# Self-attention of the second layer: softmax weights normalised before the turn, values multiplied head by head in 32-column blocks

## The reference

```python
def _L1_attn_ref(x, Wq, Wkv_down, Wk_up, Wv_up, Wo):   # N_HEADS = 8, HEAD_DIM = 32
    q = (x @ Wq.T).reshape(b, t, 8, 32)
    kv_latent = x @ Wkv_down.T                          # 64 wide
    k = (kv_latent @ Wk_up.T).reshape(b, t, 8, 32)
    v = (kv_latent @ Wv_up.T).reshape(b, t, 8, 32)
    scores = einsum('bqhd,bkhd->bhqk', q, k) * 32 ** -0.5
    attn = softmax(scores, axis=-1)
    out = einsum('bhqk,bkhd->bqhd', attn, v).reshape(b, t, 256)
    return out @ Wo.T
```

## Time and profile before

| | |
|---|---|
| median of 3 runs | 5312.76 us (5300.98 to 5316.85) |
| the profiled execution's own time | 5294.46 us |
| its span, first to last instruction | 5292.7 us |
| busy share TensorE / VectorE / ScalarE / GpSimd | 89% / 61% / 40% / 35% |
| mean granted TensorE clock | 0.935 of full speed |
| the stage of the change | about 2130 to 2432 us of the span |

### The profile page before, as it was taken

The page is one execution under the profiler, slowest core; times in us unless marked ns, Lnnn a source line. Parts: engine busy times, 40 slices in busy tenths (PEclk is TensorE's granted clock), DMA queues, the critical chain, the costliest instruction groups (busy, mean ns, idle before and its releaser), DMA issues.

```text
span 5292.7 us, 138451 instructions
## 1 busy us (share of the span) xinstructions
PE 4721.4 (89%) x48761; PEld 3730.1 (70%) x48761; DVE 3207.9 (61%) x9513; ACT 2119.9 (40%) x5243; POOL 1841.9 (35%) x2796
## 2 busy tenths in 40 slices
PE   4999999999999999896929999777999989997999
PEld 3777777779867777674627777665577768885776
DVE  4777777756546666565425666685466657764443
ACT  1444444422224444221214555342255545542333
POOL 2555555511113333334143433890034434430000
PEclk8999999999989999896968999898899998888999
DMA  6000000000000000000220100002211100005665
GB/s 201 18 18 18 18 18 18 18 1 2 1 21 29 32 28 25 0 0 20 70 63 29 36 32 28 1 0 55 58 33 32 32 21 0 0 0 114 144 143 134
DMA packets 112436, 199.69 MB, mean 38 GB/s; under 512 B 13315, under 2 KB 54659, under 8 KB 111259
## 3 DMA queue, kind: packets, MB, share of 16 engines
q1 hardware_dynamic: 108147, 188.67, 13.4%
q0 software_dynamic: 4096, 8.40, 0.6%
HBM read 183.29 MB, written 18.97 MB: 38 GB/s over the span
## 4 chain that ended last, share of the span: by engine, by line
PE 75%; DVE 7%; issue 6%; ACT 5%; POOL 4%; SPq 1%; DMA 1%; POOLq 1%; DVEq 0%; ACTq 0%
PE psum_banks L555 6%; PE psum_banks L3075 6%; PE psum_banks L3084 5%; PE psum_banks L560 5%; PE psum_banks L620 4%; PE psum_banks L664 4%; PE psum_banks L671 3%; PE psum_banks L1623 3%; PE psum_banks L624 3%; PE psum_banks L1658 2%; PE psum_banks L2103 2%; PE psum_banks L1084 2%; PE psum_banks L2770 2%; PE psum_banks L1599 2%; ACT scratch L1741 1%
## 5 line engine op out<-in xcount | busy, mean ns | idle before, releaser
L787 DVE TENSOR_REDUCE scratch<-psum_banks 128x2 f32<-128x514 f32 x768 | 531.6, 692 | 411.8 <-PE psum_banks L555 407.8
L706 ACT ACTIVATE scratch<-psum_banks 128x512 f32<-128x512 f32 x768 | 459.4, 598 | 490.0 <-PE psum_banks L565 474.4
L560 PE MATMUL psum_banks<-scratch 32*128 32x128 f32 x6144 | 639.6, 310 | 8.2 <-ACT scratch L706 6.1
L555 PE MATMUL psum_banks<-scratch 32*128 32x257 f32 x3072 | 575.2, 441 | 50.3 <-DVE scratch L788 50.0
L560 PEld LDWEIGHTS psum_banks<-scratch 32*128 32x128 f32 x6144 | 476.6, 185 | 17.5 <-ACT scratch L706 8.6
L555 PEld LDWEIGHTS psum_banks<-scratch 32*128 32x128 f32 x3072 | 253.9, 189 | 272.7 <-issue 175.9
L3084 PEld LDWEIGHTS psum_banks<-w_L_ffn_down,scratch 128*128 128x128 f32 (+1 forms) x2560 | 335.8, 193 | 156.0 <-issue 127.1
L3075 PE MATMUL psum_banks<-scratch,w_L_ffn_up 128*128 128x512 f32 (+1 forms) x752 | 382.0, 603 | 8.2 <-DVE scratch L3262 8.2
L3262 DVE TENSOR_TENSOR scratch<-scratch 128x512 f32<-128x512 f32 x304 | 210.3, 692 | 268.5 <-ACT scratch L3128 234.3
L3128 ACT ACTIVATE scratch<-psum_banks 128x512 f32<-128x512 f32 x320 | 191.0, 598 | 430.1 <-PE psum_banks L3075 430.0
L565 PE MATMUL psum_banks<-shift_T,own_batch 32*128 32x128 bf16 x3072 | 351.2, 215 | 0.0
(11 more groups left out here) (495 smaller groups left out, 12386.3 us busy)
## 6 DMA issues: line engine op xcount, KB each, us to landing
scratch<-route_T SPq DMA_DIRECT2D x136, 512.0 KB, 7.3
scratch<-in_ctx SPq DMA_DIRECT2D x99, 514.0 KB, 3.5
scratch<-in_ctx_rows SPq DMA_DIRECT2D x130, 128.0 KB, 2.0
scratch<-route_T SPq DMA_DIRECT2D x8, 1024.0 KB, 8.8
expert_rows<-in_ctx SPq DMA_DIRECT2D x10, 512.0 KB, 17.9
scratch<-expert_rows SPq DMA_DIRECT2D x16, 192.0 KB, 2.7
expert_out<-scratch SPq DMA_DIRECT2D x16, 192.0 KB, 2.1
w_L_ffn_up<-in_L_ffn_up SPq DMA_DIRECT2D x1, 2992.0 KB
```

The source lines that it names most:

```text
L555: return pe.matmul(S[:, g % 2, :], qbd[q, t.odd, (s // 2) * P:(s // 2 + 1) * P], kT_of[q, t.odd, s // 2, :], start=True, stop=True)
L560: return pe.matmul(W[:, g % 2, c * P:(c + 1) * P], kT_of[q, t.odd, b, c * P:(c + 1) * P], qbd[q, t.odd, b * P:(b + 1) * P], start=True, st ...
L706: act.activation(pT[:, b % 2, 2 * h:2 * h + 2].rearrange("p t c q -> p t (c q)"), W, ACT.Exp).then_inc(exp_ready.sem, 1)
L787: dve.tensor_reduce(parts[:, r.t.odd, 2 * h:2 * h + 2, 0, b], S, X_AXIS, ALU.max, negate=True)
```

## The change

Four things, for L1 alone:

1. VectorE multiplies the exponentials by the inverse sums of their rows (256 columns, in place) before TensorE turns them. The tensor `w` and its instruction (L1302) are gone.
2. V becomes one matmul for each head and batch: 32 matmuls with a head's values of one batch (all 128 rows of the spread `vm`, 32 columns) at rest and 32 columns of turned weights moving. The four j's of a batch write to the four 32-partition parts of PSUM. The result already has the layout channel x token. Below it is called **V'**.
3. H and VectorE's L1268 are gone; ScalarE copies V's result (128x256) straight to `outT`, as soon as `pv_done` says that it is there.
4. In TensorE's round, TU moves from behind TX to behind S. M, V', TX, PJ, S, TU, OU is the new order.

```diff
         def values(t):
             pe.wait_ge(turned_read.sem, turned_read.at(t, 1))
             pe.wait_ge(vm_ready.sem, vm_ready.at(t, 1))
-            pe.wait_ge(heads_ready.sem, heads_ready.at(t + -1, 1))
+            if kind == "L1":
+                pe.wait_ge(heads_read.sem, heads_read.at(t + -1, 1))
+            else:
+                pe.wait_ge(heads_ready.sem, heads_ready.at(t + -1, 1))
             for n in range(nt):
                 left, vm = s["pT"][:, n * P:(n + 1) * P], s["vm"][:, t.odd, :]
                 if kind == "L1":
-                    mm = pe.matmul(O[n][:, :], left, vm[:, n * 512:(n + 1) * 512], start=True, stop=True)
+                    for b in range(NB):
+                        for j in range(4):
+                            d, q = slice(32 * j, 32 * j + 32), slice(n * P + 32 * j, n * P + 32 * j + 32)
+                            at = n * P + 32 * b
+                            mm = pe.matmul(O[0][d, at:at + 32], vm[:, n * 512 + b * P + 32 * j:n * 512 + b * P + 32 * j + 32],
+                                           s["pT"][:, q], start=True, stop=True, skip_group_check=True)
...
-            if kind == "L1" and r.own:
-                turn(r.t)
             if r.after:
                 project(r.t + 2)
...
-            if r.turned:
+            if kind != "L1" and r.turned:
                 heads(r.t + -1)
...
-            if kind == "L3" and r.own:
+            if kind != "L2" and r.own:
                 turn(r.t)
...
         def take_heads(t):
-            n = 2 if kind == "L1" else 1
-            act.wait_ge(heads_written.sem, heads_written.at(t, 1))
-            act.activation(s["outT"][:, 0:n, :], OUT[:, 0:n * P].rearrange("p (t c) -> p t c", t=n), ACT.Copy
-                           ).then_inc(heads_read.sem, 1)
+            if kind == "L1":
+                act.wait_ge(pv_done.sem, pv_done.at(t, 1))
+                act.wait_ge(out_written.sem, out_written.at(t + -1, 1))
+                act.activation(s["outT"], O[0][:, 0:2 * P].rearrange("p (t c) -> p t c", t=2), ACT.Copy).then_inc(heads_read.sem, 1)
...
-            heads(r)
...
-                link(dve.tensor_tensor(w, bc(s["rr"][:, 0:8], 2, 4), bc(k.c("quad"), 1, 8), ALU.mult), r, "w")
+                dve.tensor_tensor(by_head, by_head, bc(s["rr"][:, 0:8], 2, 32), ALU.mult).then_inc(probs_ready.sem, 1)
```

More of the change, by code:

```diff
@@ L894, in chain_steps @@
         if kind == "L1":
-            return (["max"] * has.own + ["stats"] * has.third + ["rs", "rr", "w"] * has.own)
+            return (["max"] * has.own + ["stats"] * has.third + ["rs", "rr"] * has.own)
         if kind == "L2":
@@ L908, in self_attention @@
     spread = PerTile(k.sig("operands_spread"), 1) if kind != "L1" else None
-    turned_written, turned_read, pv_done, heads_ready, heads_written, heads_read, out_written, out_read = (
-        PerTile(k.sig(n), 1) for n in ("probs_T_written", "probs_T_read", "pv_done", "heads_ready", "heads_written",
-                                       "heads_read", "out_written", "out_read"))
+    turned_written, turned_read, pv_done, heads_read, out_written, out_read = (
+        PerTile(k.sig(n), 1) for n in ("probs_T_written", "probs_T_read", "pv_done", "heads_read", "out_written", "out_read"))
+    if kind == "L1":
+        exp_ready = PerTile(k.sig("exp_ready"), 1)
+    else:
+        heads_ready, heads_written = PerTile(k.sig("heads_ready"), 1), PerTile(k.sig("heads_written"), 1)
     if kind == "L1":
@@ L1081, in heads @@
             pe.wait_ge(out_read.sem, out_read.at(t + -1, 1))
[L1082 to L1085, removed]
+            for b in range(NB):
+                mm = pe.matmul(OUT[:, 0:P], s["om"][:, 0, b * P:(b + 1) * P], window(k, b), start=(b == 0), stop=(b == NB - 1),
+                               skip_group_check=True)
             mm.then_inc(heads_written.sem, 1)
@@ L1090, in output @@
             if kind == "L1":
+                pe.wait_ge(out_read.sem, out_read.at(t + -1, 1))
                 for n in range(2):
@@ L1164, in take_heads @@
         def take_heads(t):
-            n = 2 if kind == "L1" else 1
-            act.wait_ge(heads_written.sem, heads_written.at(t, 1))
-            act.activation(s["outT"][:, 0:n, :], OUT[:, 0:n * P].rearrange("p (t c) -> p t c", t=n), ACT.Copy
-                           ).then_inc(heads_read.sem, 1)
+            if kind == "L1":
+                act.wait_ge(pv_done.sem, pv_done.at(t, 1))
+                act.wait_ge(out_written.sem, out_written.at(t + -1, 1))
+                act.activation(s["outT"], O[0][:, 0:2 * P].rearrange("p (t c) -> p t c", t=2), ACT.Copy).then_inc(heads_read.sem, 1)
+            else:
+                act.wait_ge(heads_written.sem, heads_written.at(t, 1))
+                act.activation(s["outT"][:, 0, :], OUT[:, 0:P], ACT.Copy).then_inc(heads_read.sem, 1)
         def one(r):
@@ L1208, in one @@
                     act.wait_ge(scores_read.sem, scores_read.at(r.t, 1))
-                    act.activation(s["pr"][:, 0:256], s["pr"][:, 0:256], ACT.Exp).then_inc(probs_ready.sem, 1)
+                    act.activation(s["pr"][:, 0:256], s["pr"][:, 0:256], ACT.Exp).then_inc(exp_ready.sem, 1)
             if kind == "L2" and r.own:
@@ L1260, in heads @@
             t = r.t + -1
-            if kind != "L1":
-                over_sums(r)
-            dve.wait_ge(pv_done.sem, pv_done.at(t, 1))
+            over_sums(r)
             dve.wait_ge(heads_written.sem, heads_written.at(t + -1, 1))
             w = s["w"].rearrange("p u j -> p (u j)")
[L1266 to L1270, removed]
+            dve.tensor_tensor(s["om"][:, 0, :].rearrange("p (g d) -> p g d", d=hd), O[0].rearrange("p (g d) -> p g d", d=hd),
+                              bc(w, 2, hd), ALU.mult).then_inc(heads_ready.sem, 1)
         def residual(r):
@@ L1280, in one_l1 @@
             sc, pr = D[:, 0:256].rearrange("p (u k) -> p u k", k=32), s["pr"][:, 0:256]
-            nm, w = s["nm"][:, 0:8], s["w"][:, 0:8, :]
+            nm = s["nm"][:, 0:8]
             normalised(r)
@@ L1298, in one_l1 @@
             if r.own:
-                dve.wait_ge(probs_ready.sem, probs_ready.at(r.t, 1))
-                link(dve.tensor_reduce(s["rs"][:, 0:8], pr.rearrange("p (u k) -> p u k", k=32), X_AXIS, ALU.add), r, "rs")
+                dve.wait_ge(exp_ready.sem, exp_ready.at(r.t, 1))
+                by_head = pr.rearrange("p (u k) -> p u k", k=32)
+                link(dve.tensor_reduce(s["rs"][:, 0:8], by_head, X_AXIS, ALU.add), r, "rs")
                 link(dve.reciprocal(s["rr"][:, 0:8], s["rs"][:, 0:8]), r, "rr")
-                link(dve.tensor_tensor(w, bc(s["rr"][:, 0:8], 2, 4), bc(k.c("quad"), 1, 8), ALU.mult), r, "w")
+                dve.tensor_tensor(by_head, by_head, bc(s["rr"][:, 0:8], 2, 32), ALU.mult).then_inc(probs_ready.sem, 1)
             residual(r)
```

## The result

The changed kernel takes 5351.68 us (median of four runs, 5348.12 to 5353.49) against 5306.87 us for the kernel before in the same session (5300.50 to 5316.85). The ratio is 1.0078, 95% interval 1.0064 to 1.0093: slower by 0.8%, 45 us. The forecast was 5363 us, by case A: TensorE at 1.2 GHz through the whole stage.

What follows compares the result with a forecast made beforehand. The prediction took TensorE, at its granted clock, to bound the stage. Thirty rounds at 1.2 GHz add 57.2 us and the stage's end saves 6.5, +50.7 on a median of 5312.76: 5363 us, 8 in 10 within 5262 to 5388.

Steps and rivals of the forecast that it cites:

- case A: L1 stage: TensorE stays at 1.2 GHz throughout; 5363 us, its own range 5343 to 5385; chance 0.62.
- The stage is TensorE's alone, and the clock decides: L1 stage: TensorE's work sets the 8.81 us round, so work removed is gained in full if VectorE and clock keep up.
- No rise without V: L1 stage: with V and H gone, nothing in the new round lifts the clock from 1.2 GHz before the stage ends.
- a long uninterrupted stretch of full-array streaming: TensorE: what precedes a clock rise; the change removes both such stretches, V and H, from the round.
- The round: L1 stage, M to M at 1.2 GHz: steps of 9.52 us and V' of 1.4, together 10.92 us.
- four blocks at once: V' on TensorE: 16 groups of four matmuls, 0.45 us at 2.4 GHz, 0.9 at 1.2 GHz.
- the pace of issue: V' on TensorE: issue at 0.027 us per record sets the time, 1.75 us for 64.
- the third reading: V' on TensorE: loads follow one another, 0.028 us per record, 1.76 us in all and twice that at 1.2 GHz.
- The sum: L1 stage: +57.2 us over thirty rounds and -6.5 at the stage's end, together +50.7 us.
- The edits costed at nothing: ScalarE's copies and GpSimd's spread in the L1 stage: covered, no cost; 0.4 us a round each if uncovered.
- B: L1 stage: the clock rises to 2.4 GHz with the first V'; round 6.54 us, 5231 us in all; chance 0.18.
- C: L1 stage: the clock comes and goes; 5297 us with half the rounds at 1.2 GHz, 5250 to 5345; chance 0.20.

Runs made afterwards that it cites:

- experiment 5: Changed kernel with five useless full-array 512-column matmuls once, in the first round that has V'; ratio 1.0055 to the kernel before.
- experiment 4: Changed kernel with one useless full-array 512-column matmul behind V' in each round; ratio 0.9999 to the kernel before.
- experiments 3: Changed kernel with two useless full-array 512-column matmuls behind V' in each round; 5273.00 against 5295.68 us for the kernel before.
- experiment 7: Changed kernel with the two inner loops of V' swapped, so four successive matmuls use one 32-column block; 5223.74 against 5295.68 us for the kernel before.
- experiment 2: Kernel before with TU behind S and the weights divided by their sums ahead of the turn, V and H kept; ratio 1.0004 to the kernel before.
- experiment 1: Kernel before with TU alone moved behind S; ratio 1.0004 to the kernel before.
- experiment 6: Kernel before with H cut from eight matmuls to two and V kept; ratio 1.0115 to the kernel before.

## Why the prediction was right

**The stage is TensorE's alone, and the clock decides.** Right. TensorE's bound stood through the change, VectorE idles 6.24 us a round, and of the two ways that the same round could run, 6.39 us (experiment 5) and 10.52, the clock chose.

**No rise without V.** Right in its outcome, by the reading of the earlier trace rows: S and M, however dense, do not lift the clock. Experiments 4 and 5 add that the new round also brings it down when it is up, and experiments 3 and 7 that giving back streaming restores it. But the mechanism as I put it, "a long uninterrupted stretch of full-array streaming", was too narrow. In experiment 7 eight records in a row go to one block of 32 columns, a quarter of the array, and that lifts the clock, while the same 64 records on four blocks in turn don't. So a V' over the full array isn't needed. With the order two things change together, how many blocks are used in turn (four, two, one) and how long V' lasts (1.01, 1.31, 2.24 us), and the runs don't part the two. The length alone is not the rule: in experiment 4 V' and the useless matmul last 1.65 us at 2.4 GHz, longer than the 1.44 of experiment 7, with the same pause of 0.37 us in the round, and there the clock falls.

**The round, 10.92 forecast, 10.52 measured.** M 2.01 (2.00 forecast), TX to PJ 0.84 (0.84), TU 0.46 (0.44), OU 0.99 (1.07), S 3.44 (3.56). PJ was 1.77 (1.61). The term that was mis-sized is V': 1.01 us measured against 1.4. I took the middle between "four blocks at once" (0.9 at this clock) and "the pace of issue" (1.75); it is the first with 0.1 on top, and at 2.4 GHz 0.69 against my 1.2. The records start 11 ns apart on average there. One block at a time costs 1.44 us at 2.4 GHz, nearer to the pace of issue, and the third reading, loads one behind the other at 1.76 and 3.5, is too dear by 0.3 and 1.3 us even there. The pace of issue itself was read a little low: 0.24 us for eight records are 0.030 for one and not 0.027, so that end was 1.9 instead of 1.75; no case hangs on it.

**The sum.** Forecast +57.2 in thirty rounds and -6.5 at the end, +50.7. Measured +42.4 and -5.7, and 0.3 at the entry, +37.0. The rounds' 14.8 us less are 30 x 0.40 = 12.0 for the round, and 2.8 because the last of the thirty has no TX and no PJ, which I counted. At the end TU waited 1.76 us for VectorE's product, a wait that I had not listed; the two shorter V' (0.8) and ScalarE's first copy, which lay under that wait (0.47), took 1.2 us off again; 0.3 us is left for the other steps. The forecast of 5363 us was 11 us above the median, and what the whole kernel lost, 45 us, holds, by the medians, some 8 us outside the stage that I can't attribute. So there is luck in how close the forecast of the change came: +50.7 against +45 for the whole, but +37.0 for the stage that it was worked out for.

**The edits costed at nothing.** Right: experiment 2 is within 0.1% of the kernel before. TU, costed at 0.24 us a round at full clock, took 0.17 in experiment 1. The product (L1309) was forecast at 0.42 to 0.5. It is 0.43 at the end of the stage, where GpSimd is idle, and 0.65 or 1.22 in the rounds, where GpSimd's spread of the values runs beside it; 6 us of idle time cover that.

**The rivals.** B's round was 6.54 forecast and 6.39 in experiment 5, its bound by VectorE (6.27) shows as S's waits of 0.17 and 0.36. What failed B is the clock alone. C, a clock that comes and goes, is what experiments 4 and 6 look like, and its argument that a V' long enough to stream would lift the clock is what experiment 7 shows, save that nothing in that round brings it down again. That last I had wrong: in experiment 5 the clock falls with S, M and a V' of 0.7 us; in experiment 7, with a V' of 1.44 us, it does not.

**What stays open.** Why one full matmul beside the fast V', which makes a round as long as one block at a time (6.97 and 6.81 us), does not hold the clock where the slow V' does. That the clock is what was lost is shown; what in V' or around it decides on the clock is not. Also whether H or the absence of a pause held it in the kernel before, since experiment 6 changed both.

## What to carry to other kernels

Before taking work out of a TensorE-bound stage, find the stretches that precede each rise of the granted clock, and ask what is left of them afterwards; price the new round at both clocks. If short or packed matmuls are all that is left, try first to spread them out in time (here by swapping two loops, so that successive matmuls share one column block) rather than adding work for nothing. In this kernel that was 1.4% faster than before, useless matmuls 0.5% faster, and the packed order 0.8% slower. An order that makes one step faster by itself is only better if the clock stays.

## What was not expected of the hardware

- 64 records of 32 columns at rest and 32 moving take, at 1.2 GHz, 1.01 us over four column blocks in turn, 1.31 over two and 2.24 on one; at 2.4 GHz 0.69 and 1.44 for four and one. The Trainium skill ("TensorEngine Tiling (Array Packing)", Instruction Overhead) gives each matmul about 60 cycles; spread over four blocks the 64 show 26 cycles each (0.69 us / 64 = 11 ns at 2.4 GHz), so the trace does not agree for packed matmuls. On one block it is 54 (22.5 ns), near it; at 1.2 GHz the two are 19 and 42 cycles.
- In the changed kernel the granted clock stayed at half from 2123 to 2577 us, with TensorE 96% busy in the stage itself, and it rose in the same stage for a version with the same instructions in another order (experiment 7).
- VectorE's product over 128x256 (L1309) took 0.43 us alone and up to 1.22 beside GpSimd.
